# Graph attention with layer norm: the eight large additions and products at a group's end on GpSimd, and VectorE's comparisons one quad ahead

## The chip, the core and the metric

The kernel runs on one core of one Trainium2 chip. The metric is the device time of that core in microseconds (us): 1753.01 us, the median of three runs (1748.39 to 1753.73). One further execution was taken by the profiler.

## The reference

```python
x, adj: (8192, 128) f32, (8192, 8192) int32 of zeros and ones; 4 heads of 32 channels
Wh        = (x @ W.T) split by head
score_src = einsum('knd,kd->kn', Wh, a1);  score_dst = einsum('knd,kd->kn', Wh, a2)
e         = leaky_relu(score_src[:, :, None] + score_dst[:, None, :], 0.2)
e         = where(adj == 0, -inf, e)
alpha     = softmax(e, axis=-1)
h_prime   = einsum('kij,kjd->kid', alpha, Wh)
out       = layernorm(x + h_prime)      # over the 128 channels, eps 1e-5
```

## The kernel before

The exponential of the leaky ReLU is a product of a row factor and a column factor on either side of score_src + score_dst = 0, so for each pair of nodes the kernel needs only the edge and the sign of that sum. `step` holds the edges on the steep side, `rest` the other edges, both as one-byte matrices. TensorE multiplies `step` with `G` (three bf16 parts of the weighted values) and `rest` with `F` (two fp16 parts) and sums in six PSUM banks.

The output rows are taken in 16 groups of 512. For each group the kernel goes through 16 quads: 512 source nodes, four blocks of 128. One quad, numbered k over the whole kernel, goes through the engines so:

- SyncE loads one MB of `adj`, four buffers deep (`load_adj`).
- GpSimd makes `step` tiles of five of the 16 (block, head) pairs (line 325), then packs the `adj` block of quad k+2 to bytes (`take_edges`, line 302); that waits until TensorE has transposed quad k.
- TensorE transposes the packed block of quad k+2 into one of two PSUM banks (line 644) after VectorE has made `rest` of quad k, and before its own 64 `F` products of quad k.
- ScalarE makes nine `step` tiles (line 397).
- VectorE makes the last two (line 505), reading the transposed edges in PSUM. `take_step` then masks the 14 others with the edges in two instructions (lines 510 and 512), and `take_rest` makes `rest` by an exclusive or (line 522).
- TensorE multiplies (line 657): 64 products with `G` after `step_set`, 64 with `F` after `rest_set`.

`step` has four buffers and `rest` two. Every engine runs its own instruction list in the written order, and semaphores tie the lists together. Before the comparisons of quad k GpSimd also waits for `quad_past`, which VectorE raises at the end of a quad, k-1 times.

At the end of a group TensorE closes the six banks (line 672). ScalarE copies them to `late` after its comparisons of quad 1 of the next group (`take_sums`, line 381). VectorE then runs `finish` of the group before as a generator, one piece after each quad from quad 1 on: two additions of the partial sums (545, 546), a product with beta and an addition (549, 550), a product with alpha (553), an addition (556), maximum and reciprocal (559, 562), the product into `y` (566), the residual (571), the statistics (575, 580, 584). GpSimd raises the variance to the power -1/2 (306), VectorE makes the shift (589), ScalarE scales (`normalise`, 387), and SyncE stores. After the last group all this stands alone at the end. Every second group VectorE and ScalarE run through one body of a loop, TensorE and GpSimd have theirs unrolled.

Of the kernel before, what the change touches and what calls it, by code (L numbers as in the profile page):

```python
# [6 lines left out]
def gat_layernorm(nc, x, adj, W, a, out):  # L7
# [12 lines left out]
    ALU = mybir.AluOpType  # L20
# [3 lines left out]
    P = 128  # L24
    N, D_IN = x.shape
    HEADS, D_OUT = a.shape[0], a.shape[1] // 2
# [38 lines left out]
    with ctx:  # L65
# [3 lines left out]
        def sem(name):  # L69
            return ctx.enter_context(nc.semaphore(name))  # L70
# [93 lines left out]
        quad_past = sem("quad_past")  # L164
        pool_compared = sem("pool_compared")
        step_set = sem("step_set")
        rest_set = sem("rest_set")
        rest_done = sem("rest_done")
# [1 line left out]
        acc_act = sem("acc_act")  # L170
        res_loaded = sem("res_loaded")
        var_set = sem("var_set")
        rstd_set = sem("rstd_set")
        shift_set = sem("shift_set")
        y_set = sem("y_set")
# [16 lines left out]
        LEAD = 4  # L192


        SCALED = 14

        def done(n):
            return n + LEAD
# [72 lines left out]
        def _(pool):  # L271
# [25 lines left out]
            def take_edges(k):  # L297
# [3 lines left out]
                    pool.wait_ge(transposed, k - N8 + 1)  # L301
                nc.gpsimd.tensor_scalar(edge[:, k % N8], adj_t[:, k % NA], 1.0, -1.0, ALU.min, ALU.max).then_inc(edge_set, 1)  # L302

            def inverse_deviation(g):
                pool.wait_ge(var_set, done(g + 1))
                nc.gpsimd.tensor_tensor(rstd[:, :], mv[:, :, 1], half_t[:, :], ALU.pow).then_inc(rstd_set, 1)  # L306
# [108 lines left out]
        def _(dve):  # L415
# [79 lines left out]
            dve.wait_ge(part_set, done(3 * (JB // TJ)))  # L495
            dve.wait_ge(f_set, JB // TJ)

            def take_step(g, q, n):

                nth = at(dve, quad_no(g, q) + 1)  # L500
                if q == 0:
                    dve.wait_ge(s_loaded[n], 8 * (g + 2 - n))
                dve.wait_ge(transposed, nth)
                for b, h in DVE_TILES:
                    nc.vector.scalar_tensor_tensor(step_u8[:, q % NS, h, b // E, :, b % E], s_all[:, n, h],  # L505
                                                   d_neg[:, q * IB + b, h:h + 1], edgeT8[q % 2][:, b // E, :, b % E],
                                                   ALU.is_ge, ALU.logical_and)
                dve.wait_ge(act_compared, nth)
                dve.wait_ge(pool_compared, nth)
                nc.vector.scalar_tensor_tensor(step[:, q % NS, 0:HEADS - 1], edgeT[q % 2][:, 0:HEADS - 1], ONES,  # L510
                                               step[:, q % NS, 0:HEADS - 1], ALU.bitwise_and, ALU.bitwise_and)
                nc.vector.scalar_tensor_tensor(step[:, q % NS, HEADS - 1, 0:WORDS // U], edgeT[q % 2][:, HEADS - 1, 0:WORDS // U],  # L512
                                               ONES, step[:, q % NS, HEADS - 1, 0:WORDS // U], ALU.bitwise_and, ALU.bitwise_and
                                               ).then_inc(step_set, 1)


            def take_rest(g, q, waits=True):
# [7 lines left out]
            CHAIN0, CHAIN_STEP = links[0], 10  # L525

            def finish(g):

                got = [0]

                def then(ins):
                    got[0] += 1
                    ins.then_inc(dve_chain, 1)

                def wait_last():
                    dve.wait_ge(dve_chain, CHAIN0 + g * CHAIN_STEP + got[0])

                rows = bass.ds(g * IB, IB)

                def per_row(v, width):  # L540
                    return v.rearrange("p b h -> p (b h)").unsqueeze(2).to_broadcast([P, CHUNKS, width])

                top, low = acc_sb[:, :, 0:HC], acc_sb[:, :, BC:BC + HC]
                dve.wait_ge(acc_act, done((g + 2) * BANKS))
                nc.vector.tensor_tensor(low, low, acc_sb[:, :, BC + HC:CH], ALU.add)
                then(nc.vector.tensor_tensor(top, top, acc_sb[:, :, HC:2 * HC], ALU.add))
                yield
                wait_last()
                nc.vector.tensor_tensor(low, low, per_row(beta[:, rows, :], HC), ALU.mult)
                then(nc.vector.tensor_tensor(top, top, acc_sb[:, :, 2 * HC:BC], ALU.add))  # L550
                yield
                wait_last()
                then(nc.vector.tensor_tensor(top, top, per_row(alpha[:, rows, :], HC), ALU.mult))
                yield
                wait_last()
                then(nc.vector.tensor_tensor(top, top, low, ALU.add))
                yield
                wait_last()
# [3 lines left out]
                then(nc.vector.reciprocal(rden[:, :, :], rden[:, :, :]))  # L562
                yield
                wait_last()
                dve.wait_ge(stored, 16 * done(g))
                then(nc.vector.tensor_tensor(y.rearrange("p b (h c) -> p (b h) c", h=HEADS), top[:, :, 0:D_OUT],  # L566
                                             per_row(rden[:, :, :], D_OUT), ALU.mult))
                yield
                wait_last()
                dve.wait_ge(res_loaded, 16 * g + 16)  # L570
                then(nc.vector.tensor_tensor(y, y, res, ALU.add))  # L571
                yield
                wait_last()
# [11 lines left out]
                for _ in range(2):  # L585
                    yield
                assert got[0] == CHAIN_STEP
                dve.wait_ge(rstd_set, g + 1)
                nc.vector.scalar_tensor_tensor(shift[:, :], mv[:, :, 0], -1.0, rstd[:, :], ALU.mult, ALU.mult  # L589
                                               ).then_inc(shift_set, 1)  # L590

            def group(g, n, first=False, last=False):
                closing = iter(()) if first else finish(g - 1)
                for q in range(QUADS):
                    take_step(g, q, n)
                    take_rest(g, q, waits=not first or q >= NL)
                    if q > 0:
                        next(closing, None)
                    dve.sem_inc(quad_past, 1)  # L599
                for _ in closing:  # L600
                    pass

            group(0, 0, first=True)
            with dve.Fori(0, GROUPS // 2 - 1) as u:
                g = 2 * u + 1
# [110 lines left out]
```

## Time and profile before

| what | value |
|---|---|
| median of 3 runs | 1753.01 us |
| the profiled execution, its time | 1744.82 us |
| its span | 1743.0 us |
| VectorE busy | 1649.7 us, 95% |
| ScalarE busy | 1549.6 us, 89% |
| TensorE matmul busy | 1459.4 us, 84% |
| GpSimd busy | 1430.3 us, 82% |
| mean granted TensorE clock | 0.954 |

Busy time is the sum of the durations of an engine's instructions, so it tells how full the engine is. What one instruction costs in a row of them is read from start to start, since the next begins a little before the last has ended. Idle time with its releaser tells which semaphore ended it; "issue" is time in which the engine waited for nothing that the profile shows.

### The profile page before, as it was taken

The numbers are of one execution on the slowest core, as the hardware profiler recorded it, in microseconds if no ns is written. First come the engines' busy times: TensorE is split into PE (matmuls) and PEld (weight loads), VectorE is DVE, ScalarE is ACT, GpSimd is POOL, SyncE is SP. The second block draws the span as 40 slices with busy tenths as digits, with TensorE's granted clock in tenths as the row PEclk, the third lists the DMA queues.
The fourth block names the chain that finished last, engine by engine and source line by source line (L and its number), as shares of the span: only waits on it lengthen the run. The fifth ranks groups of instructions, "written<-read, shape, count | busy, mean of one in ns | idle before, by whom it ended". The sixth has DMA issues, their size and how long they took to land.

```text
span 1743.0 us, 80201 instructions
## 1 busy us (share of the span) xinstructions
PE 1459.4 (84%) x35235; PEld 1412.6 (81%) x35235; DVE 1649.7 (95%) x1856; ACT 1549.6 (89%) x2567; POOL 1430.3 (82%) x1582
## 2 busy tenths in 40 slices
PE   6306989989889889988889898998898998998886
PEld 4106988988888888988888888988888988888886
DVE  3697999999999999999999999999999999999997
ACT  3368999998999999899899999899998989999994
POOL 0039978989899888988899898989888898989983
PEclk9757999999999999999999999999999999999998
DMA  2505665656556575656557475555657565665530
GB/s 75 146 0 195 196 186 179 197 191 196 183 172 209 170 208 171 200 181 198 180 171 224 156 216 177 193 186 180 193 167 204 179 193 181 197 201 164 193 124 20
DMA packets 161762, 303.05 MB, mean 174 GB/s; under 512 B 9680, under 2 KB 22096, under 8 KB 161424
## 3 DMA queue, kind: packets, MB, share of 16 engines
q1 hardware_dynamic: 161424, 298.03, 54.5%
q8 instruction: 275, 4.51, 1.0%
q14 instruction: 63, 0.52, 0.1%
HBM read 293.67 MB, written 4.33 MB: 171 GB/s over the span
## 4 chain that ended last, share of the span: by engine, by line
DVE 39%; issue 29%; PE 17%; ACT 7%; POOL 4%; DMA 1%; DVEq 1%; SPq 0%; ACTq 0%; POOLq 0%
DVE step L510 17%; PE bank L657 14%; DVE step L505 12%; ACT step L397 6%; DVE step L512 3%; POOL step L325 3%; PE bank L644 1%; DMA xr<-in_x 1%; DVE F L488 1%; POOL edge L302 1%; DVE rest L522 1%; DVE stats L575 1%; ACT F L368 1%; DVE xr L571 1%; DVE xr L566 1%
## 5 line engine op out<-in xcount | busy, mean ns | idle before, releaser
L397 ACT ACTIVATE step<-s_all,sd 128x512 uint8<-128x512 f32 x2304 | 1423.1, 721 | 44.1 <-PE bank L657 43.9
L325 POOL TENSOR_SCALAR step<-s_all,sd 128x512 uint8<-128x512 f32 x1280 | 915.7, 734 | 113.1 <-DVEq L599 111.9
L657 PE MATMUL bank<-G,step 128*128 128x99 bf16 x16384 | 791.6, 209 | 138.8 <-DVE step L512 98.9
L657 PEld LDWEIGHTS bank<-G,step 128*128 128x128 fp8e4 x16384 | 751.8, 98 | 163.4 <-DVE step L512 122.2
L522 DVE SCALAR_TENSOR_TENSOR rest<-step,bank 128x2048 int32<-128x2048 int32 x256 | 585.7, 2288 | 10.1
L657 PE MATMUL bank<-F,rest 128*128 128x66 f16 x16384 | 556.5, 195 | 20.7 <-issue 20.7
L657 PEld LDWEIGHTS bank<-F,rest 128*128 128x128 fp8e4 x16384 | 537.1, 98 | 21.9 <-issue 21.9
L302 POOL TENSOR_SCALAR edge<-adj_t 128x2048 int8<-128x2048 int32 x256 | 484.6, 1893 | 58.4 <-PE bank L644 56.4
L510 DVE SCALAR_TENSOR_TENSOR step<-bank,step 128x1536 int32<-128x1536 int32 x256 | 447.5, 1748 | 3.2 <-ACT step L397 3.2
L505 DVE SCALAR_TENSOR_TENSOR step<-s_all,sd,bank 128x512 uint8<-128x512 f32 x512 | 358.9, 743 | 20.2 <-PE bank L644 9.9
L644 PE MATMUL bank<-identb,edge 128*128 128x128 bf16 x2048 | 159.1, 221 | 79.6 <-POOL edge L302 79.5
L644 PEld LDWEIGHTS bank<-identb,edge 128*128 128x128 bf16 x2048 | 125.1, 99 | 81.0 <-issue 80.0
L512 DVE SCALAR_TENSOR_TENSOR step<-bank,step 128x256 int32<-128x256 int32 x256 | 105.4, 412 | 0.0
L381 ACT COPY late<-bank 128x495 f32<-128x495 f32 x96 | 42.7, 552 | 59.7 <-PE bank L672 59.7
L286 POOL PARTITION_ALL_REDUCE d_max<-d_part x1 | 0.4, 389 | 62.6 <-DVE d_part L439 62.6
L433 DVE COPY G<-bank 128x256 f32 x32 | 13.4, 420 | 38.7 <-PE bank L637 38.7
L294 POOL TENSOR_TENSOR late<-late,G 128x528 f32<-128x528 f32 x8 | 10.5, 1336 | 44.7 <-ACT G L366 23.9
L387 ACT ACTIVATE xr<-xr,shift,rstd 128x128 f32<-128x128 f32 x64 | 26.2, 480 | 9.0 <-DVE shift L589 9.0
L306 POOL TENSOR_TENSOR rstd<-mv,half_t 128x4 f32<-128x4 f32 x16 | 16.3, 1019 | 21.7 <-DVE mv L584 21.7
L352 ACT COPY step<-bank 4x512 f32<-4x512 f32 x16 | 9.2, 574 | 24.5 <-PE bank L637 16.0
L366 ACT CAST G<-step 128x528 f32 x24 | 15.5, 648 | 15.8 <-DVE step L492 13.8
L366 ACT CAST G<-late 128x528 f32 x24 | 15.2, 647 | 13.6 <-DVE late L492 5.6
(78 smaller groups left out, 393.0 us busy)
## 6 DMA issues: line engine op xcount, KB each, us to landing
adj_t<-in_adj SPq DMA_DIRECT2D x512, 512.0 KB, 4.8
s_all<-sT_scratch SPq DMA_DIRECT2D x16, 1024.0 KB, 10.2
xr<-in_x SPq DMA_DIRECT2D x32, 256.0 KB, 3.1
out<-xr SPq DMA_DIRECT2D x16, 256.0 KB, 5.5
sT_scratch<-step SPq DMA_DIRECT2D x16, 8.0 KB
a_blk<-in_L_gnn_a SPq DMA_DIRECT2D x8, 0.1 KB, 1.7
step<-in_L_gnn_W SPq DMA_DIRECT2D x1, 64.0 KB, 1.8
```

Source lines behind the costliest of these rows:

```text
L302: nc.gpsimd.tensor_scalar(edge[:, k % N8], adj_t[:, k % NA], 1.0, -1.0, ALU.min, ALU.max).then_inc(edge_set, 1)
L325: last = nc.gpsimd.tensor_scalar(step_u8[:, k % NS, h, n // E, :, n % E], s_all[:, g % 2, h], STEEP, d_steep[:, q * IB + n, h:h + 1], ALU. ...
L366: last = nc.scalar.copy(G[:, blk, :, part, :], wide[n][:, :, :, 0])
L381: nc.scalar.copy(late[:, b * USED:b * USED + n_ch * CH], acc[b][:, 0:n_ch * CH]).then_inc(acc_act, 1)
L387: last = nc.scalar.activation(y[:, b], y[:, b], ACT.Identity, scale=rstd[:, b:b + 1], bias=shift[:, b:b + 1])
L397: last = nc.scalar.activation(step_u8[:, q % NS, h, b // E, :, b % E], s_all[:, n, h], ACT.Sigmoid, scale=STEEP, bias=d_steep[:, q * IB + ...
L505: nc.vector.scalar_tensor_tensor(step_u8[:, q % NS, h, b // E, :, b % E], s_all[:, n, h], d_neg[:, q * IB + b, h:h + 1], edgeT8[q % 2][:, ...
L510: nc.vector.scalar_tensor_tensor(step[:, q % NS, 0:HEADS - 1], edgeT[q % 2][:, 0:HEADS - 1], ONES, step[:, q % NS, 0:HEADS - 1], ALU.bitwi ...
L512: nc.vector.scalar_tensor_tensor(step[:, q % NS, HEADS - 1, 0:WORDS // U], edgeT[q % 2][:, HEADS - 1, 0:WORDS // U], ONES, step[:, q % NS, ...
L522: nc.vector.scalar_tensor_tensor(rest[:, q % NL], step[:, q % NS], ONES, edgeT[q % 2], ALU.bitwise_xor, ALU.bitwise_and).then_inc(rest_set, 1)
L644: last = nc.tensor.transpose(edgeT16[q % 2][:, u, b * P:(b + 1) * P], edge16[:, q % N8, b, u * P:(u + 1) * P], identb[:, :])
L657: last = nc.tensor.matmul(acc[k][:, col:col + width], matrix[:, h, n // E, b * P:(b + 1) * P, n % E], values[:, q * IB + n, h].rearrange(" ...
```

## The change

Eight `tensor_tensor` instructions of `finish` go from VectorE to GpSimd as `close(g, part)`, one after the `take_edges` of each of the quads in `CLOSING`. VectorE keeps maximum, reciprocal, statistics and shift, in quads 8, 11, 12 and 13. The power goes from quad 11 to quad 13 of GpSimd's list, `normalise` from quad 14 to quad 15 of ScalarE's. New semaphores (`low_set`, `top_set`, `rden_set`, `sum_set`) carry the chain across the two engines. GpSimd no longer waits for `quad_past`. VectorE's two comparisons are a function of their own, `compare`, that stands for quad q+1 between `take_step` and `take_rest` of quad q. Of the two masking instructions the small one comes first.

```diff
-        SCALED = 14
+        CLOSING = (2, 3, 4, 5, 6, 7, 9, 10)
+        SCALED = 15
+            def close(g, part):
+                if part == 0:
+                    pool.wait_ge(acc_act, done((g + 2) * BANKS))
+                    nc.gpsimd.tensor_tensor(low, low, acc_sb[:, :, BC + HC:CH], ALU.add).then_inc(low_set, 1)
+                elif part == 1:
+                    nc.gpsimd.tensor_tensor(top, top, acc_sb[:, :, HC:2 * HC], ALU.add).then_inc(top_set, 1)
...
+                elif part == 6:
+                    pool.wait_ge(rden_set, g + 1)
+                    pool.wait_ge(stored, 16 * done(g))
+                    nc.gpsimd.tensor_tensor(y.rearrange("p b (h c) -> p (b h) c", h=HEADS), top[:, :, 0:D_OUT],
+                                            per_row(rden[:, :, :], D_OUT), ALU.mult).then_inc(sum_set, 1)
+                else:
+                    pool.wait_ge(sum_set, 2 * g + 1)
+                    pool.wait_ge(res_loaded, 16 * g + 16)
+                    nc.gpsimd.tensor_tensor(y, y, res, ALU.add).then_inc(sum_set, 1)
...
                     k = quad_no(g, q)
-                    if k > 1:
-                        pool.wait_ge(quad_past, k - 1)
...
-                    if q == 11 and g > 0:
+                    if q in CLOSING and g > 0:
+                        close(g - 1, CLOSING.index(q))
+                    if q == 13 and g > 0:
                         inverse_deviation(g - 1)
+            for part in range(len(CLOSING)):
+                close(GROUPS - 1, part)
             inverse_deviation(GROUPS - 1)
...
                 for q in range(QUADS):
-                    take_step(g, q, n)
+                    take_step(g, q)
+                    if q + 1 < QUADS:
+                        compare(g, q + 1, n)
+                    elif not last:
+                        compare(g + 1, 0, 1 - n)
                     take_rest(g, q, waits=not first or q >= NL)
-                    if q > 0:
+                    if q >= 8:
                         next(closing, None)
-                    dve.sem_inc(quad_past, 1)
```

VectorE's list in quad 2 of a group before, with the piece of the group's end that follows it; L505 is a comparison, L510 and L512 mask, L522 makes `rest`.

```order
L505 SCALAR_TENSOR_TENSOR step<-s_all,sd,bank 128x512 [waits transposed]
L505 SCALAR_TENSOR_TENSOR step<-s_all,sd,bank 128x512
L510 SCALAR_TENSOR_TENSOR step<-bank,step 128x1536 [waits pool_compared,act_compared]
L512 SCALAR_TENSOR_TENSOR step<-bank,step 128x256
L522 SCALAR_TENSOR_TENSOR rest<-step,bank 128x2048 [waits rest_done,step_set]
L536 ISA
L549 ISA [waits dve_chain]
L549 TENSOR_TENSOR late<-late,beta 128x16x33
L550 TENSOR_TENSOR late<-late 128x16x33
```

The same place in the changed kernel; L559 masks, L547 are the comparisons of quad 3, L570 makes `rest` of quad 2.

```order
L559 SCALAR_TENSOR_TENSOR step<-bank,step 128x256 [waits pool_compared,act_compared,dve_compared]
L559 SCALAR_TENSOR_TENSOR step<-bank,step 128x1536
L545 REGISTER_ALU
L547 SCALAR_TENSOR_TENSOR step<-s_all,sd,bank 128x512 [waits transposed]
L547 SCALAR_TENSOR_TENSOR step<-s_all,sd,bank 128x512
L570 SCALAR_TENSOR_TENSOR rest<-step,bank 128x2048 [waits rest_done,step_set]
```

The large additions and products are gone from here, and the wait for the transposed edges of the next quad stands before `rest` of this one.

GpSimd's list in quads 1 and 2 of a group before:

```order
L325 TENSOR_SCALAR step<-s_all,sd 128x512 [waits rest_done,quad_past]
L325 TENSOR_SCALAR step<-s_all,sd 128x512 x4
L302 TENSOR_SCALAR edge<-adj_t 128x2048 [waits transposed,adj_loaded3]
L325 TENSOR_SCALAR step<-s_all,sd 128x512 [waits rest_done,quad_past]
L325 TENSOR_SCALAR step<-s_all,sd 128x512 x4
L302 TENSOR_SCALAR edge<-adj_t 128x2048 [waits transposed,adj_loaded0]
```

The changed kernel there, in quads 2 and 3; L320 and L322 are the first two parts of `close`.

```order
L364 TENSOR_SCALAR step<-s_all,sd 128x512 [waits rest_done]
L364 TENSOR_SCALAR step<-s_all,sd 128x512 x4
L308 TENSOR_SCALAR edge<-adj_t 128x2048 [waits transposed,adj_loaded0]
L320 TENSOR_TENSOR late<-late 128x16x33 [waits acc_act]
L364 TENSOR_SCALAR step<-s_all,sd 128x512 [waits rest_done]
L364 TENSOR_SCALAR step<-s_all,sd 128x512 x4
L308 TENSOR_SCALAR edge<-adj_t 128x2048 [waits transposed,adj_loaded1]
L322 TENSOR_TENSOR late<-late 128x16x33
```

Each part stands between the packing of quad k+2 and the comparisons of quad k+1, and `quad_past` is gone.

## Rows read from the trace of the kernel before

**Rows 1.** The page: busy time of each engine, and the chain by engine.
```profile
PE 1459.4 (84%) x35235; PEld 1412.6 (81%) x35235; DVE 1649.7 (95%) x1856; ACT 1549.6 (89%) x2567; POOL 1430.3 (82%) x1582
...
DVE 39%; issue 29%; PE 17%; ACT 7%; POOL 4%; DMA 1%; DVEq 1%; SPq 0%; ACTq 0%; POOLq 0%
```

**Rows 2.** Timeline of VectorE, one quad without an end piece: start, us, instruction.
```profile
908.87 1.40 DVE L505 SCALAR_TENSOR_TENSOR step<-s_all,sd,bank 128x512 uint8<-128x512 f32 x2
910.18 1.75 DVE L510 SCALAR_TENSOR_TENSOR step<-bank,step 128x1536 int32<-128x1536 int32 x1
911.85 0.41 DVE L512 SCALAR_TENSOR_TENSOR step<-bank,step 128x256 int32<-128x256 int32 x1
912.30 2.29 DVE L522 SCALAR_TENSOR_TENSOR rest<-step,bank 128x2048 int32<-128x2048 int32 x1
914.50 1.40 DVE L505 SCALAR_TENSOR_TENSOR step<-s_all,sd,bank 128x512 uint8<-128x512 f32 x2
```

**Rows 3.** Line 672, TensorE closing the banks: durations, first and last start.
```profile
L672 PE MATMUL bank<-zeros,identb x96: 166/167/169, 237.1 to 1728.5; 128*128 128x2 bf16 x96
```

**Rows 4.** Timeline of VectorE after the last quad.
```profile
1729.74 0.71 DVE L545 TENSOR_TENSOR late<-late 128x528 f32<-128x528 f32 x1 [3.93 <-ACT late L381]
...
1733.95 0.17 DVE L559 TENSOR_SCALAR rden<-late 128x16 f32<-128x16 f32 x1
...
1734.44 0.69 DVE L566 TENSOR_TENSOR xr<-late,rden 128x512 f32<-128x512 f32 x1
...
1735.89 0.87 DVE L575 BATCH_NORM_STATS2 stats<-xr 128x6 f32<-128x128 f32 x4
...
1737.21 0.17 DVE L584 TENSOR_SCALAR mv<-mv 128x4 f32<-128x4 f32 x1
1738.52 0.16 DVE L589 SCALAR_TENSOR_TENSOR shift<-mv,rstd 128x4 f32<-128x4 f32 x1 [1.14 <-POOL rstd L306]
```

**Rows 5.** Timeline of GpSimd in the middle of the kernel.
```profile
841.98 4.39 POOL L325 TENSOR_SCALAR step<-s_all,sd 128x512 uint8<-128x512 f32 x5 [0.31 <-DVEq L599]
...
902.63 1.02 POOL L306 TENSOR_TENSOR rstd<-mv,half_t 128x4 f32<-128x4 f32 x1
...
908.87 3.38 POOL L325 TENSOR_SCALAR step<-s_all,sd 128x512 uint8<-128x512 f32 x5
...
914.09 3.38 POOL L325 TENSOR_SCALAR step<-s_all,sd 128x512 uint8<-128x512 f32 x5
```

**Rows 6.** Line 294 on GpSimd: ns of one at least, median, at most.
```profile
L294 POOL TENSOR_TENSOR late<-late,G x8: 1149/1222/1670, 86.2 to 132.5; 128x528 f32<-128x528 f32 x8
```

**Rows 7.** Timeline of ScalarE.
```profile
834.22 2.67 ACT L381 COPY late<-bank 128x495 f32<-128x495 f32 x6 [4.23 <-PE bank L672]
...
906.45 5.63 ACT L397 ACTIVATE step<-s_all,sd 128x512 uint8<-128x512 f32 x9 [0.63 <-PE bank L657]
911.98 1.63 ACT L387 ACTIVATE xr<-xr,shift,rstd 128x128 f32<-128x128 f32 x4
```

**Rows 8.** Timeline of TensorE, from quad 1 of a group on.
```profile
841.72 0.66 PE L657 MATMUL bank<-G,step 128*128 128x99 bf16 x11
847.38 3.79 PE L657 MATMUL bank<-G,step 128*128 128x99 bf16 x53 [5.00 <-issue]
851.00 0.61 PE L644 MATMUL bank<-identb,edge 128*128 128x128 bf16 x8
...
853.42 3.01 PE L657 MATMUL bank<-G,step 128*128 128x99 bf16 x64
856.26 0.61 PE L644 MATMUL bank<-identb,edge 128*128 128x128 bf16 x8
...
858.68 3.01 PE L657 MATMUL bank<-G,step 128*128 128x99 bf16 x64
```

**Rows 9.** Waits: engine and line, what it waited for: us, times, longest.
```profile
POOL step L325 <- DVEq L599: 111.9, 88, 3.5
...
PE bank L657 <- issue: 58.6, 27, 5.6
```

More of the change, by code:

```diff
@@ L163, in gat_layernorm @@
         act_compared = sem("act_compared")
-        quad_past = sem("quad_past")
         pool_compared = sem("pool_compared")
+        dve_compared = sem("dve_compared")
         step_set = sem("step_set")
@@ L172, in gat_layernorm @@
         var_set = sem("var_set")
+        low_set = sem("low_set")
+        top_set = sem("top_set")
+        rden_set = sem("rden_set")
+        sum_set = sem("sum_set")
         rstd_set = sem("rstd_set")
@@ L302, in take_edges, with per_row @@
                 nc.gpsimd.tensor_scalar(edge[:, k % N8], adj_t[:, k % NA], 1.0, -1.0, ALU.min, ALU.max).then_inc(edge_set, 1)
+            def close(g, part):
+                top, low = acc_sb[:, :, 0:HC], acc_sb[:, :, BC:BC + HC]
+                def per_row(v, width):
+                    return v.rearrange("p b h -> p (b h)").unsqueeze(2).to_broadcast([P, CHUNKS, width])
+                rows = slice(g * IB, (g + 1) * IB)
+                if part == 0:
[3 more added lines that the diff above has]
+                    nc.gpsimd.tensor_tensor(top, top, acc_sb[:, :, HC:2 * HC], ALU.add).then_inc(top_set, 1)
+                elif part == 2:
+                    pool.wait_ge(low_set, 2 * g + 1)
+                    nc.gpsimd.tensor_tensor(low, low, per_row(beta[:, rows, :], HC), ALU.mult).then_inc(low_set, 1)
+                elif part == 3:
+                    pool.wait_ge(top_set, 4 * g + 1)
+                    nc.gpsimd.tensor_tensor(top, top, acc_sb[:, :, 2 * HC:BC], ALU.add).then_inc(top_set, 1)
+                elif part == 4:
+                    pool.wait_ge(top_set, 4 * g + 2)
+                    nc.gpsimd.tensor_tensor(top, top, per_row(alpha[:, rows, :], HC), ALU.mult).then_inc(top_set, 1)
+                elif part == 5:
+                    pool.wait_ge(top_set, 4 * g + 3)
+                    pool.wait_ge(low_set, 2 * g + 2)
+                    nc.gpsimd.tensor_tensor(top, top, low, ALU.add).then_inc(top_set, 1)
+                elif part == 6:
[7 more added lines that the diff above has]
+                    nc.gpsimd.tensor_tensor(y, y, res, ALU.add).then_inc(sum_set, 1)
             def inverse_deviation(g):
@@ L496, in _, with compare @@
             dve.wait_ge(f_set, JB // TJ)
-            def take_step(g, q, n):
-                nth = at(dve, quad_no(g, q) + 1)
+            def compare(g, q, n):
                 if q == 0:
                     dve.wait_ge(s_loaded[n], 8 * (g + 2 - n))
-                dve.wait_ge(transposed, nth)
+                dve.wait_ge(transposed, at(dve, quad_no(g, q) + 1))
                 for b, h in DVE_TILES:
-                    nc.vector.scalar_tensor_tensor(step_u8[:, q % NS, h, b // E, :, b % E], s_all[:, n, h],
-                                                   d_neg[:, q * IB + b, h:h + 1], edgeT8[q % 2][:, b // E, :, b % E],
-                                                   ALU.is_ge, ALU.logical_and)
+                    last = nc.vector.scalar_tensor_tensor(step_u8[:, q % NS, h, b // E, :, b % E], s_all[:, n, h],
+                                                          d_neg[:, q * IB + b, h:h + 1], edgeT8[q % 2][:, b // E, :, b % E],
+                                                          ALU.is_ge, ALU.logical_and)
+                last.then_inc(dve_compared, 1)
@@ L508, in take_step @@
+            def take_step(g, q):
+                nth = at(dve, quad_no(g, q) + 1)
+                dve.wait_ge(dve_compared, nth)
                 dve.wait_ge(act_compared, nth)
                 dve.wait_ge(pool_compared, nth)
[L510 to L514, printed above, removed]
+                for part in ((slice(HEADS - 1, HEADS), slice(0, WORDS // U)), (slice(0, HEADS - 1), slice(0, WORDS))):
+                    last = nc.vector.scalar_tensor_tensor(step[:, q % NS, part[0], part[1]], edgeT[q % 2][:, part[0], part[1]],
+                                                          ONES, step[:, q % NS, part[0], part[1]],
+                                                          ALU.bitwise_and, ALU.bitwise_and)
+                last.then_inc(step_set, 1)
@@ L523, in take_rest @@
                                                ALU.bitwise_xor, ALU.bitwise_and).then_inc(rest_set, 1)
-            CHAIN0, CHAIN_STEP = links[0], 10
+            CHAIN0, CHAIN_STEP = links[0], 3
             def finish(g):
@@ L536, in wait_last @@
                     dve.wait_ge(dve_chain, CHAIN0 + g * CHAIN_STEP + got[0])
[L538 to L558, printed above, removed]
+                top = acc_sb[:, :, 0:HC]
+                dve.wait_ge(top_set, 4 * g + 4)
                 then(nc.vector.tensor_scalar(rden[:, :, :], top[:, :, D_OUT].rearrange("p (b h) -> p b h", h=HEADS),
@@ L561, in finish @@
                 wait_last()
[L562 to L573, printed above, removed]
+                nc.vector.reciprocal(rden[:, :, :], rden[:, :, :]).then_inc(rden_set, 1)
+                for _ in range(3):
+                    yield
+                dve.wait_ge(sum_set, 2 * g + 2)
                 for b in range(IB):
@@ L584, in finish @@
                 nc.vector.tensor_scalar(mv[:, :, 1], mv[:, :, 1], EPS, None, ALU.add).then_inc(var_set, 1)
-                for _ in range(2):
+                assert got[0] == CHAIN_STEP
+                for _ in range(1):
                     yield
-                assert got[0] == CHAIN_STEP
                 dve.wait_ge(rstd_set, g + 1)
@@ L594, in group @@
                 for q in range(QUADS):
-                    take_step(g, q, n)
+                    take_step(g, q)
[3 more added lines that the diff above has]
+                        compare(g + 1, 0, 1 - n)
                     take_rest(g, q, waits=not first or q >= NL)
-                    if q > 0:
+                    if q >= 8:
                         next(closing, None)
-                    dve.sem_inc(quad_past, 1)
                 for _ in closing:
                     pass
+            compare(0, 0, 0)
             group(0, 0, first=True)
```

## Prediction, written before the changed kernel was run

> **What bounds the kernel now.** I read the page first: VectorE is busy for 95% of the span and heads the chain, while ScalarE, TensorE and GpSimd have 11 to 18% left [rows 1]. Then VectorE's timeline. Between pieces of a group's end a quad takes 914.50 - 908.87 = 5.63 us, back to back: comparisons 1.31, the large mask 1.67, the small mask 0.45, `rest` 2.20 [rows 2]. The small mask lasts 0.41 us, and instructions here overlap by about 0.08, so it should take 0.33; the other 0.12 us is the wait of `rest` for `step_set`, raised by the instruction just ahead. A group: the banks are closed from 237.1 to 1728.5 us, six times a group, and the six of one group lie 1.7 us apart, so 15 groups take 1489.7 us and one takes 99.3 [rows 3]. Sixteen quads are 90.1 of these; 9.2 remain for the group's end and for waits. So VectorE sets the pace, and a microsecond taken from it counts until the next engine is full.
>
> **What the change takes from VectorE.** The eight moved instructions take 1733.95 - 1729.74 = 4.21 and 1735.89 - 1734.44 = 1.45 us in the tail, 5.7 together [rows 4]; in the groups they also lose some to waits. The 0.12 us for `step_set` goes from each quad, since 1.3 us of comparisons now stand between: 1.9 per group. What stays is 0.49 (maximum, reciprocal), 1.49 (from 1735.89 to the end of the one at 1737.21) and 0.16 for the shift, 2.1 in all [rows 4]. VectorE alone then needs 16 x 5.51 + 2.1 = 90.3 us a group, and I add 0.3 for the loop's turn (an estimate): 90.6.
>
> **What it gives to GpSimd.** A quad there takes 914.09 - 908.87 = 5.22 us, 83.5 for sixteen, and the power 1.0 [rows 5]. Eight `tensor_tensor` come on top. The nearest row is line 294 with the same 16 runs of 33 numbers per partition: 1.15 us at least, 1.22 median, 1.67 at most, the longer ones while VectorE itself had two-input work [rows 6]. None of that is beside the moved parts now, so I take 1.15: 9.2 us. Below it the price could only fall to VectorE's own 0.7 (5.66/8, [rows 4]); above, to 1.67. GpSimd alone: 83.5 + 1.0 + 9.2 = 93.7 us, more than VectorE. Its present waits for `quad_past`, 111.9 us [rows 9], go, but they were not what held VectorE, so I count nothing for them; their cover is that GpSimd still cannot pack quad k+2 before quad k is transposed.
>
> The row at 841.98 shows five comparisons in 4.39 us instead of 3.38, while VectorE ran its two-input additions [rows 5]. The Trainium skill (SBUF — State Buffer, Who interferes with whom) says that a VectorE instruction with two SBUF inputs holds off a GpSimd one that reads SBUF, and that one with a single SBUF input does not. By that rule, the trace agrees (1.0 us), the stretching goes with the move, and the price of a part is its undisturbed one; without the rule I would take the median, 1.22, and the group would be 0.6 us longer.
>
> **What the new order costs.** Call T the end of a quad's masks on VectorE. TensorE needs 2.84 us for 64 products with `G`, 0.45 for transposes and 1.97 for `F`, 5.26 in all when it never waits (853.42 to 858.68 in [rows 8]; the transposes are complete 0.61 after they start). In the new list `rest` is ready at T + 1.3 + 2.2 = T + 3.5, the transposes for quad q+2 are done at T + 4.2, and VectorE wants them at T + 5.5. So 1.3 us of room is left. Before, VectorE wanted them only after the next `rest`: TensorE had them at T + 3.5 and VectorE came at T + 7.9, 4.4 us of room, and 5.6 with an end piece of 1.2 ahead. That matters because TensorE stands still once per group, in the `G` products of quad 1: 5.00 us in the row shown, and the 53 products behind it take 851.00 - 847.38 = 3.62 us where 53/64 of 2.84 is 2.35, so 1.3 more [rows 8]. All such stops come to 58.6 us [rows 9], 3.9 per group. Nearly all of it used to be hidden in those 5.6 us. Now TensorE is late by 3.6 (the large one) + 1.3 = 4.9, of which VectorE sees 4.9 - 1.3 = 3.6 us. VectorE: 90.6 + 3.6 = 94.2.
>
> GpSimd meets the same stop, since packing quad 5 waits for the transposes of quad 3. How far ahead it is decides. From part 7 (quad 10) on it gains 0.3 us per quad on VectorE, and 2.1 from what VectorE kept, and pays 1.0 for the power, so at quad 3, after the first part, it is about 2.1 us ahead of the masks. Its packing could then start at T1 + 8.9 - 2.1 = T1 + 6.8 (T1 is T of quad 1), and the transposes are done at T1 + 4.2 + 4.9 = T1 + 9.1: 2.3 us lost. Another 0.3 I give to the power, whose variance now comes only in quad 12. GpSimd: 93.7 + 2.6 = 96.3 us a group. The parts cost it 0.85 us per quad net against VectorE, so the lead is gone by about quad 8, and from there VectorE waits for `pool_compared`, about 2 us a group in all. That is the same sum seen from VectorE: 94.2 + 2.1 = 96.3.
>
> ScalarE: nine tiles take 911.98 - 906.45 = 5.53 us, sixteen quads 88.5, copies of the banks 2.5 (2.67 less the overlap), scaling 1.5 [rows 7]; 92.5 without waits. It comes under 96.3 with 3.8 us for its waits at the banks (4.23 in the row shown) and for the shift, which now comes only two quads ahead of use.
>
> **The sum**, against the profiled execution's 1744.8 us (span 1743.0): 15 groups by 99.3 - 96.3 = 3.0 each, -45; group 0, which has no end work, by 16 x 0.11 (ScalarE's 5.53 is next), -2; the tail, where eight parts at 1.15 plus about 0.05 of semaphore each replace 5.7, +4. Together -43, 1702. The median of the runs shown lies 8.2 us above the profiled execution, so I forecast 1753 - 43 = 1710 us. Low end: a GpSimd that never waits, 93.7, gives -84 - 2 + 4 = -82, 1671. High end with the parts at 1.67: +4.2 a group and +4 in the tail makes +24, 1777; that needs the disturbed price where nothing disturbs, so I let the range reach only half of that way.
>
> **Rivals.**
> 1. The stop of TensorE is hidden after all (GpSimd comes to it with no lead, or the stop moves to a place with more room). GpSimd then gives 94 to 94.5 a group, -75, 1678. For it: packing at zero lead begins at T3 - 0.2 - 1.9 (T3 that of quad 3), well behind the transposes. Against: the trace shows this stop in the same quad of nearly every group. 0.2.
> 2. ScalarE becomes the bound and keeps its waits. Its rows show 4.23 us at the banks and 0.63 in one quad [rows 7]; 92.5 + 4.2 + several 0.6 is 98.5, and the gain is 15 x 0.8 + 2 - 4 = 10, 1743. If it stays at 4.23 alone it is 96.7, my forecast. Against: its waits are those of an engine that is ahead, and they shrink when the others speed up. 0.1.
> 3. Slower. GpSimd cannot store up any lead, because packing is tied to the transposes two quads back and these to `rest`. Then every part counts in full against VectorE: 8 x (1.15 - 0.3) = 6.8, with the stop 3.6, 90.6 + 10.4 = 101.0 a group, +26 - 2 + 4 = +28, 1781. It decides from 8.6 us of waits per group on VectorE (99.2 less 90.6). For it: 1.3 us of room instead of 4.4. Against: the ring lets GpSimd be nearly one quad ahead, and 88 waits on `quad_past` show that it gets there [rows 9]. 0.08.
> 4. A part costs much more than line 294, as a product with a broadcast operand or into `y` might; at 1.55 us a part the gain is gone, at 1.67 it is the 1777 above. 0.07.
>
> The Trainium skill (GPSIMD Engine Reference, Elementwise — side-by-side cycle accounting) speaks against such a move: it gives GpSimd about 2.6 cycles per element with two inputs and calls VectorE twice as fast. Its figures make 528 elements an estimated 1.14 us; line 294's 1.15 agrees. By it the two engines' sum grows, and the move pays only through GpSimd's idle share.
>
> **Chances.** Forecast 0.55; rivals 0.2, 0.1, 0.08, 0.07. A measurement of this kernel tells about 0.3%, 5 us, from no change. Faster by more: forecast, the first, most of the second: 0.83. Within: 0.06. Slower: 0.11. The range, 1680 to 1748, takes in most of the first two rivals.
>
> **What would show it.** Right: a group of 96 to 97 us; quads of 5.5 us on VectorE with no gap ahead of `rest`; parts of 1.12 to 1.25 us; comparisons on GpSimd at 3.38 everywhere; VectorE waiting for TensorE's transposes about once a group, 2 to 5 us, near quad 3, and for GpSimd in quads 7 to 11; GpSimd the fullest engine with VectorE. Wrong: parts above 1.4 us (rival 4), ScalarE ending VectorE's waits (2), waits of VectorE over 8 us a group (3), or no wait for transposes at all (1).

## The result, and the profile after

The changed kernel takes 1712.59 us, the median of four runs (1706.65 to 1714.83), against 1751.72 us of the kernel before beside it; the ratio is 0.9774, 95% interval [0.9753, 0.9795]. The forecast was 1710 us. The two profiled executions lie 1744.8 - 1714.8 = 30 us apart, less than the medians' 39: the one of before was faster than all four of its runs, the one of after was the slowest of its four. What follows explains those 30 us.

The page after, answering [rows 1]:

```profile
PE 1462.5 (85%) x35235; PEld 1411.8 (82%) x35235; DVE 1558.9 (91%) x1728; ACT 1544.6 (90%) x2567; POOL 1521.7 (89%) x1710
...
POOL 34%; DVE 21%; PE 20%; issue 15%; ACT 7%; DMA 1%; DVEq 0%; SPq 0%; ACTq 0%; POOLq 0%
```

GpSimd has taken the head of the chain. The banks of the groups are now closed like this (line 672 of before is line 697), answering [rows 3]:

```profile
L697 PE MATMUL bank<-zeros,identb x96: 166/167/169, 241.9 to 1694.8; 128*128 128x2 bf16 x96
```

1694.8 - 241.9 - 1.7 over 15 is 96.7 us a group; it was 99.3 and was forecast at 96.3. Group 0 ends 4.8 us later than before, the tail behind the last bank went from 14.5 to 18.2 us. The 15 groups bring -38.5 us, and -38.5 + 4.8 + 3.7 gives the 30.

VectorE in a quad without an end piece, answering [rows 2] (start, duration; two merged masks, two comparisons, `rest`):

```profile
824.37 2.08 DVE L559 SCALAR_TENSOR_TENSOR step<-bank,step 128x256 int32<-128x256 int32 x2
826.37 1.39 DVE L547 SCALAR_TENSOR_TENSOR step<-s_all,sd,bank 128x512 uint8<-128x512 f32 x2
827.68 2.27 DVE L570 SCALAR_TENSOR_TENSOR rest<-step,bank 128x2048 int32<-128x2048 int32 x1
829.88 2.08 DVE L559 SCALAR_TENSOR_TENSOR step<-bank,step 128x256 int32<-128x256 int32 x2
```

A quad is 5.51 us, as forecast, and nothing stands ahead of `rest`. Three of the eight parts on GpSimd, by line: shortest, median, longest in ns, answering [rows 6]:

```profile
L320 POOL TENSOR_TENSOR late<-late x16: 1122/1142/1153, 250.5 to 1696.1; 128x528 f32<-128x528 f32 x16
...
L335 POOL TENSOR_TENSOR late<-late x16: 1317/1348/1367, 289.2 to 1701.7; 128x528 f32<-128x528 f32 x16
...
L344 POOL TENSOR_TENSOR xr<-xr x16: 1261/1281/1286, 307.6 to 1704.7; 128x512 f32<-128x512 f32 x16
```

The eight sum to 9.3 us (1.06 to 1.35 each), 9.2 was forecast. A product with a broadcast operand is no dearer than a sum. The comparisons on GpSimd fell from 734 to 699 ns in the mean.

TensorE's stop, at its worst, on the three engines that feel it (one fence for each engine; the brackets give the idle time and what ended it). TensorE:

```profile
250.25 0.43 PE L682 MATMUL bank<-G,step 128*128 128x99 bf16 x6
256.13 5.01 PE L682 MATMUL bank<-G,step 128*128 128x99 bf16 x58 [5.45 <-issue]
260.94 1.05 PE L669 MATMUL bank<-identb,edge 128*128 128x128 bf16 x8
```

VectorE:

```profile
252.01 2.08 DVE L559 SCALAR_TENSOR_TENSOR step<-bank,step 128x256 int32<-128x256 int32 x2
262.02 1.41 DVE L547 SCALAR_TENSOR_TENSOR step<-s_all,sd,bank 128x512 uint8<-128x512 f32 x2 [7.93 <-PE bank L669]
```

GpSimd:

```profile
251.58 3.39 POOL L364 TENSOR_SCALAR step<-s_all,sd 128x512 uint8<-128x512 f32 x5
262.15 1.89 POOL L308 TENSOR_SCALAR edge<-adj_t 128x2048 int8<-128x2048 int32 x1 [7.18 <-PE bank L669]
```

VectorE wants the transposed edges of quad 3 at 254.1 and gets them at 262.0; GpSimd cannot pack before the same transposes are done. The stop also slows what follows it: from 256.1 to 261.0 the granted clock was 0.50, which is 1.2 GHz, after TensorE had stood still for 5.45 us, and the 58 products behind the stop took 4.8 us (260.94 - 256.13) where 58/64 of 2.84 is 2.6. In a group with a 2.69 us stop (TensorE goes on at 846.39) the clock behind it was 1.00, and the waits are 1.31 and 0. The waits in all (us, times, longest), answering [rows 9]:

```profile
DVE step L547 <- PE bank L669: 72.3, 30, 7.9
PE bank L682 <- issue: 70.6, 43, 5.4
...
POOL edge L308 <- PE bank L669: 44.1, 22, 7.2
...
POOL rstd L348 <- DVE mv L605: 8.2, 16, 1.6
...
POOL xr L339 <- DVE rden L591: 7.4, 16, 1.2
...
DVE step L559 <- POOL step L364: 6.6, 9, 0.9
```

The last row is the one that was not foreseen: VectorE hardly waits for GpSimd's comparisons. What took that time shows in quad 8. VectorE, then GpSimd:

```profile
881.63 1.46 DVE L588 TENSOR_SCALAR rden<-late 128x16 f32<-128x16 f32 x1
883.12 0.25 DVE L591 RECIPROCAL rden<-rden 128x16 f32<-128x16 f32 x1
```
```profile
881.15 1.91 POOL L308 TENSOR_SCALAR edge<-adj_t 128x2048 int8<-128x2048 int32 x1
883.46 1.06 POOL L339 TENSOR_TENSOR xr<-late,rden 128x512 f32<-128x512 f32 x1 [0.40 <-DVE rden L591]
```

The maximum over 16 numbers took 0.17 us before [rows 4]; now it ends just as GpSimd's packing does, at 883.1. Its median is 1452 ns, that of the shift 897 (187 before). Not every group pays that: in the mean of the 15 groups the maximum lasts 1.07 us longer than before and the shift 0.58.

### The profile page after: what moved, and what is told of

Read it like the earlier page. It is cut to its first block, busy times and chain, and to the rows that moved or that the text cites. A ratio compares the mean times of both kernels' runs of the same rounds, so it can differ in the third digit from the quotient of the medians.

```text
span 1713.0 us, 79627 instructions
## 1 busy us (share of the span) xinstructions
PE 1462.5 (85%) x35235; PEld 1411.8 (82%) x35235; DVE 1558.9 (91%) x1728; ACT 1544.6 (90%) x2567; POOL 1521.7 (89%) x1710
## 4 chain that ended last, share of the span: by engine, by line
POOL 34%; DVE 21%; PE 20%; issue 15%; ACT 7%; DMA 1%; DVEq 0%; SPq 0%; ACTq 0%; POOLq 0%
POOL step L364 20%; PE bank L682 17%; POOL edge L308 10%; DVE rest L570 7%; DVE step L559 6%; ACT step L440 5%; DVE step L547 5%; PE bank L669 2%; DMA xr<-in_x 1%; DVE F L531 1%; POOL xr L344 1%; DVE stats L596 1%; ACT F L411 1%; POOL late L328 1%; POOL late L325 1%
## 5 line engine op out<-in xcount | busy, mean ns | idle before, releaser
L364 POOL TENSOR_SCALAR step<-s_all,sd 128x512 uint8<-128x512 f32 x1280 | 865.8, 699 | 0.0
L570 DVE SCALAR_TENSOR_TENSOR rest<-step,bank 128x2048 int32<-128x2048 int32 x256 | 583.4, 2279 | 0.0
L559 DVE SCALAR_TENSOR_TENSOR step<-bank,step 128x256 int32<-128x256 int32 (+1 forms) x512 | 532.2, 1080 | 12.8 <-POOL step L364 6.6
L308 POOL TENSOR_SCALAR edge<-adj_t 128x2048 int8<-128x2048 int32 x256 | 485.3, 1896 | 44.3 <-PE bank L669 44.1
L547 DVE SCALAR_TENSOR_TENSOR step<-s_all,sd,bank 128x512 uint8<-128x512 f32 x512 | 358.2, 742 | 72.6 <-PE bank L669 72.3
L669 PEld LDWEIGHTS bank<-identb,edge 128*128 128x128 bf16 x2048 | 121.0, 99 | 138.0 <-issue 80.6
L424 ACT COPY late<-bank 128x495 f32<-128x495 f32 x96 | 41.9, 526 | 11.2 <-PE bank L697 11.2
L320 POOL TENSOR_TENSOR late<-late 128x528 f32<-128x528 f32 x16 | 18.3, 1141 | 11.8 <-ACT late L424 11.8
L588 DVE TENSOR_SCALAR rden<-late 128x16 f32<-128x16 f32 x16 | 18.7, 1168 | 10.9 <-POOL late L335 10.9
```

Of the source, the lines that this page charges most:

```text
L424: nc.scalar.copy(late[:, b * USED:b * USED + n_ch * CH], acc[b][:, 0:n_ch * CH]).then_inc(acc_act, 1)
L547: last = nc.vector.scalar_tensor_tensor(step_u8[:, q % NS, h, b // E, :, b % E], s_all[:, n, h], d_neg[:, q * IB + b, h:h + 1], edgeT8[q % ...
L559: last = nc.vector.scalar_tensor_tensor(step[:, q % NS, part[0], part[1]], edgeT[q % 2][:, part[0], part[1]], ONES, step[:, q % NS, part[0 ...
L669: last = nc.tensor.transpose(edgeT16[q % 2][:, u, b * P:(b + 1) * P], edge16[:, q % N8, b, u * P:(u + 1) * P], identb[:, :])
```

## The experiments

All were timed in three rounds beside the kernel before; ratios are to it, and differences in us between two versions are taken from their ratios unless a subtraction is written out. Of each edit the central lines are shown; `...` marks lines left out between them. "Stop" is short for TensorE's standing still, once a group.

**order_only**: the kernel before with the new order on VectorE alone (the small mask first, as in the changed kernel).

```diff
-                    take_step(g, q, n)
+                    take_step(g, q)
+                    if q + 1 < QUADS:
+                        compare(g, q + 1, n)
+                    elif not last:
+                        compare(g + 1, 0, 1 - n)
                     take_rest(g, q, waits=not first or q >= NL)
```

> The kernel before with only the new order on VectorE (comparisons of quad q+1 between the masks and rest of quad q); the group's end stays on VectorE and GpSimd keeps its wait for quad_past. Theory A (the stop of TensorE once a group, which the old order hid, now reaches VectorE): the 1.9 us per group saved at step_set are given back by a wait of VectorE for the transposes of about 2 us, group 99 to 99.8 us, 1745 to 1758 us, nearly no change. Rival B (the order is a gain by itself): 15 x 1.9 + 2 = 30 us less, 1720 us.

1747.64 us, 0.9986 [0.9969, 1.0004]: no change that can be told. VectorE's waits for the transposes rose from 9.9 us to

```profile
DVE step L505 <- PE bank L655: 39.8, 17, 5.4
```

which is about what 16 x 1.9 at `step_set` had given, 30 us. Theory A holds.

**move_only**: the changed kernel with VectorE's old order.

```diff
-                    take_step(g, q)
-                    if q + 1 < QUADS:
-                        compare(g, q + 1, n)
-                    elif not last:
-                        compare(g + 1, 0, 1 - n)
+                    take_step(g, q, n)
```

> The changed kernel with VectorE's old order (comparisons of quad q just ahead of its masks); the eight additions and products are on GpSimd and quad_past is gone. Theory A (GpSimd is full at 93.7 us a group plus its waits, and the old order leaves VectorE 4.4 us of room for TensorE's stop): VectorE needs 92.5 us alone, GpSimd 93.7 + 1.5 to 2.5, group 95.3 to 96.5, 1700 to 1715 us, as fast as the changed kernel or a little faster. Rival B (the order brings its 1.9 us per group): about 98.5 a group, 1740 us.

1719.98 us, 0.9824 [0.9806, 0.9841], 5 us above the expected span. So the move brings 1.8 points of the 2.3, and the order about half a point on top, far less than rival B's.

**with_quad_past**: the changed kernel with GpSimd's wait for `quad_past` put back.

```diff
                     k = quad_no(g, q)
+                    if k > 1:
+                        pool.wait_ge(quad_past, k - 1)
```

> The changed kernel with GpSimd's wait for quad_past put back. Theory A (GpSimd's lead is bounded anyway by the transposes two quads back): the lead it may store falls by at most about 2 us; GpSimd is the full engine, so each wait counts: 0 to 2 us a group, 1712 to 1742 us. Rival B (the pacing was not binding): 1712, no wait on DVEq in the trace. A third view (the removed pacing is what made the change pay, as GpSimd needs its lead for the eight parts): over 3 us a group, above 1757 us.

1718.71 us, 0.9811 [0.9789, 0.9833]. That is about 6 us above the changed kernel, at the edge of what the intervals tell apart. GpSimd's comparisons never waited for `quad_past`:

```profile
L367 POOL TENSOR_SCALAR step<-s_all,sd 128x512 uint8<-128x512 f32 x1280 | 865.4, 698 | 0.0
```

That is the sign of rival B: taking this wait out was not what made the change pay.

**split_s**: the load of a group's scores in four parts.

```diff
-            def load_s(g, n):
-                src = sT_v[g].unsqueeze(0).to_broadcast([P, HEADS, ROWS])
-                sync.dma_start(s_all[:, n], src).then_inc(s_loaded[n], 16)
+            def load_s(g, n, heads=range(HEADS)):
+                for h in heads:
+                    src = sT_v[g, h:h + 1].unsqueeze(0).to_broadcast([P, 1, ROWS])
+                    sync.dma_start(s_all[:, n, h:h + 1], src).then_inc(s_loaded[n], 16)
...
-                    if q == 6 and g + 1 < GROUPS:
+                    if q in (6, 8, 10, 12) and g + 1 < GROUPS:
```

> The changed kernel with the one load of a group's scores (s_all, 1 MB) split by head into four loads, after the adjacency loads of quads 6, 8, 10 and 12. Theory A (TensorE's stop in quad 1 is instruction fetch that queues behind this load): the stops fall from 65 us to under 25 in all and no longer sit in quad 1; VectorE's 72 us of waits for transposes and GpSimd's 44 fall by more than half; group 94 to 95, 1680 to 1695 us. Rival B (the stop belongs to that place in TensorE's instruction list whatever the DMAs do): same stops, 1712 us. Rival C (the small loads are slower in sum): 1720 us.

1676.11 us, 0.9580 [0.9559, 0.9602]. Waits and bank closings:

```profile
DVE step L560 <- POOL step L365: 23.5, 36, 0.9
...
PE bank L683 <- issue: 14.0, 26, 1.6
DVE step L548 <- PE bank L670: 13.3, 10, 5.3
```
```profile
L698 PE MATMUL bank<-zeros,identb x96: 166/167/169, 236.1 to 1654.9; 128*128 128x2 bf16 x96
```

The long stops are gone, and a group is (1654.9 - 236.1 - 1.7) / 15 = 94.5 us. That is GpSimd's list with no wait for TensorE in the groups: 83.5 + 1.0 + 9.3, and 0.8 for its waits for the reciprocal and the variance, 94.6. Theory A holds for the load; that instruction fetch is what waits behind it is not shown. The stop cost the changed kernel 2.2 us a group, and 5.8 us in group 0, which ends at 236.1 instead of 241.9. The mean granted clock rose from 0.955 to 0.968; this is a part of the stop's price.

**before_split_s** and **order_only_split_s**: the same edit on the kernel before, and on order_only.

> The kernel before with the score load split by head into four loads, after the adjacency loads of quads 6, 8, 10 and 12; nothing else. Theory A (the old order hid TensorE's stop almost whole, and the new order is worth its 1.9 us per group once the stop is gone): 98.4 to 99.3 a group, 1735 to 1750 us, so that order_only_split_s (1717.6) lies 20 to 30 us below it. Rival B (the new order is worth nothing in itself): 1718 us, as with the new order.

> The kernel before with the new order on VectorE, and with the score load split by head into four loads, after the adjacency loads of quads 6, 8, 10 and 12. Theory A (the order alone gave nothing because TensorE's stop took back what step_set gave): without the stop the 1.9 us per group appear, and the part of the stop that was not hidden; group 96.4 to 97.2, 1700 to 1718 us. Rival B (the order has no gain, its 1.9 us are lost for another reason, as by waits of TensorE): group 98.5, 1738 us.

before_split_s: 1734.12 us, 0.9915 [0.9898, 0.9931], a hair under the expected span. order_only_split_s: 1717.60 us, 0.9826 [0.9795, 0.9856], at its upper end. So the order alone is worth 16 us without the stop, less than the 20 to 30 expected, and nothing with it. And the stop costs the kernel before 15 us, the changed kernel 0.9774 - 0.9580, 34 us.

**move_only_split_s**: move_only with the load in four parts.

> The changed kernel with VectorE's old order, and with the score load split as in split_s. Theory A (GpSimd is full at 94.4 us a group once the stop is gone, and VectorE's old order needs 92.5 plus 1.5 to 2 us in which its maximum and its shift wait for GpSimd): 94.4 to 95.5 a group, 1676 to 1692 us, little behind split_s's 1676. Rival B (the order brings its 1.9 us per group in full): 96.3, 1705 us.

1680.34 us, 0.9605 [0.9589, 0.9621]. That is 4 us above split_s, and the intervals overlap: with GpSimd full, the new order gives little even without the stop. With the stop it gave 9 (0.9824 - 0.9774).

**late_s**: the changed kernel, the load whole but at quad 10 of SyncE's list.

```diff
-                    if q == 6 and g + 1 < GROUPS:
+                    if q == 10 and g + 1 < GROUPS:
```

> The changed kernel with the one undivided score load issued after the adjacency load of quad 10 instead of quad 6. Theory A (the load makes the stop): TensorE's long stops move from quad 1 to about quad 5 of a group, with their sum (60 us) unchanged; GpSimd has less lead there and waits less for the transposes, 1700 to 1713 us. Rival B (the stop belongs to quad 1 of TensorE's list): the stops stay in quad 1 and the time at 1712 us.

1681.79 us, 0.9611 [0.9595, 0.9628], far below either expectation. The long stops ended 31 to 36 us after a group's last bank instead of 11 to 15, and they sum to less. The longest, on TensorE, and GpSimd beside it:

```profile
652.52 4.01 PE L682 MATMUL bank<-G,step 128*128 128x99 bf16 x46 [4.76 <-issue]
656.33 0.84 PE L669 MATMUL bank<-identb,edge 128*128 128x128 bf16 x8
```
```profile
651.20 3.40 POOL L364 TENSOR_SCALAR step<-s_all,sd 128x512 uint8<-128x512 f32 x5
657.33 1.89 POOL L308 TENSOR_SCALAR edge<-adj_t 128x2048 int8<-128x2048 int32 x1 [2.73 <-PE bank L669]
```

All waits:

```profile
PE bank L682 <- issue: 51.1, 42, 4.8
...
DVE step L547 <- PE bank L669: 39.3, 26, 6.3
```

This stop of 4.76 us holds GpSimd for 2.73. Stops of 3.34 to 3.62 us held it for 1.8 to 2.6 in the changed kernel, and those of 3.35 and 3.38 here not at all; its waits for transposes fall from 44.1 to 9.8 us. So the load makes the stop, and its place decides much of what it costs. GpSimd's rows fit the prediction's picture of a lead that the parts use up: at the worst stop of the changed kernel it was through with its comparisons at 254.97, 1.2 us before TensorE went on, with one part made; here at 654.60, 2.1 us after, with five made. How much of the gain comes from that, and how much from the shorter stops, no run tells. The direction was expected; that 28 of the stop's 34 us would go was not.

**gpsimd_extra** and **vectore_extra**: the changed kernel with work added on one engine whose result is used by nothing; first GpSimd's edit, behind the dots VectorE's.

```diff
+                    if q == 8 and g > 0:
+                        nc.gpsimd.tensor_tensor(spare[:, :, :],
+                                                alpha[:, :, :].rearrange("p j h -> p (j h)").unsqueeze(1).to_broadcast([P, 2, JB * HEADS]),
...
+                for b in range(IB):
+                    nc.vector.bn_stats(spare[:, b], y[:, b])
```

> The changed kernel with one more addition of 512 numbers per partition (about 1.1 us) on GpSimd in quad 8 of each of 15 groups; its result is used by nothing. Theory A (GpSimd is the full engine of the changed kernel): all of it counts, 15 x 1.1 = 16 us, 1728 us. Rival B (VectorE with the waits for transposes sets the pace): 1712 to 1717 us.

> The changed kernel with the four bn_stats of a group made twice on VectorE (0.87 us more per group, the copy used by nothing). Theory A: it stands in quad 11, where VectorE else waits for GpSimd, so 0 to 5 us, 1712 to 1717 us. Rival B (VectorE sets the pace): 16 x 0.87 = 14 us, 1726 us.

gpsimd_extra: the addition took 1.29 us, 19 in all, and the kernel 1732.20 us, 0.9900 [0.9871, 0.9930]: 22 us more, so all of it counts. vectore_extra: 1721.93 us, 0.9841 [0.9825, 0.9858], 12 of the 14 us added. That is outside Theory A's 1712 to 1717 and under rival B's 1726. The trace shows the way it takes, on GpSimd:

```profile
POOL rstd L349 <- DVE mv L608: 20.1, 16, 2.4
```

against 8.2 us. The statistics are not beside GpSimd's work: the power stands in its list in quad 13 and waits for them with all comparisons of the later quads behind it. GpSimd is the full engine, and this is one of the places where VectorE's time enters its list.

**split_s_max**: split_s with the maximum on GpSimd.

```diff
                     nc.gpsimd.tensor_tensor(top, top, low, ALU.add).then_inc(top_set, 1)
+                    pool.wait_ge(top_set, 4 * g + 4)
+                    nc.gpsimd.tensor_scalar(rden[:, :, :], top[:, :, D_OUT].rearrange("p (b h) -> p b h", h=HEADS),
+                                            TINY, None, ALU.max).then_inc(max_set, 1)
```

> split_s with the maximum of the row sums (16 numbers per partition) on GpSimd after the sixth part, so that VectorE keeps only the reciprocal there. Theory A (VectorE's 0.17 us maximum took 1.45 us because GpSimd's edge packing held the shared SBUF port, which also delayed the seventh part on GpSimd by 0.4 us; GpSimd is the full engine): GpSimd pays about 0.15 and gets 0.4 back, group 94.1 to 94.4, 1671 to 1677 us; VectorE's extra 1.3 us are gone, and the reciprocal stays at 0.25. Rival B (VectorE sets the pace even here): 16 x 1.3 = 20 us less, 1655 us. Rival C (the port delay moves to the reciprocal): 1676 us with a reciprocal above 1 us.

1672.92 us, 0.9560 [0.9544, 0.9576]. The reciprocal stays at 0.25 us; VectorE's 1.3 us turn into waits for the comparisons (42.0 us instead of 23.5), and the group stays at 94.4. Theory A holds; in time the version can't be told from split_s. Its median is the lowest of all versions.

**split_s_max_residual**: this with the residual's addition back on VectorE, in quad 11 ahead of the statistics; the eighth part leaves GpSimd's list.

```diff
+                dve.wait_ge(sum_set, g + 1)
+                dve.wait_ge(res_loaded, 16 * g + 16)
+                then(nc.vector.tensor_tensor(y, y, res, ALU.add))
+                wait_last()
```

> split_s_max with the residual's addition moved back to VectorE, ahead of its statistics in quad 11. Theory A (GpSimd is full, 94.3 us a group, with a residual of 1.28; VectorE has about 2 to 3 us left): group 93.0 to 93.3, ScalarE's 92.5 next; 1655 to 1662 us. Rival B (VectorE's two-input addition and GpSimd hold each other off at the shared port and give back what was moved): 1671 to 1677 us.

1762.83 us, 1.0075 [1.0058, 1.0092], slower than the kernel before by 0.75%. VectorE, then GpSimd:

```profile
908.99 6.89 DVE L593 TENSOR_TENSOR xr<-xr 128x512 f32<-128x512 f32 x1
915.91 0.87 DVE L596 BATCH_NORM_STATS2 stats<-xr 128x6 f32<-128x128 f32 x4
```
```profile
908.23 1.89 POOL L310 TENSOR_SCALAR edge<-adj_t 128x2048 int8<-128x2048 int32 x1
910.10 3.38 POOL L365 TENSOR_SCALAR step<-s_all,sd 128x512 uint8<-128x512 f32 x5
913.44 1.90 POOL L310 TENSOR_SCALAR edge<-adj_t 128x2048 int8<-128x2048 int32 x1
923.00 1.03 POOL L349 TENSOR_TENSOR rstd<-mv,half_t 128x4 f32<-128x4 f32 x1 [7.67 <-DVE mv L605]
```

An addition that takes 0.69 us in the tail of this run lasted 6.89, and so in 13 of the 15 groups (6.16 and 6.39 us in the other two). It ended 0.55 us after GpSimd's last instruction at 915.3, through seven of them that followed each other without a gap, and none of the seven was stretched. GpSimd then stood 7.67 us for the variance, in all

```profile
POOL rstd L349 <- DVE mv L605: 117.3, 16, 7.7
```

against 8.2 us in split_s_max. 109 us of new waits less 15 x 1.28 for the part that left GpSimd is 90, and the kernel lost 1762.83 - 1672.92 = 90 us. Rival B holds, in a size that nobody expected, and one-sided: only VectorE was held off. Why it was held through all seven is open: GpSimd also ran without a gap beside a 1.98 us product of the kernel before, which came in behind one instruction (below).

## Why the prediction was right, and where its steps were off

- **VectorE's quad**: 5.51 us, as worked out. **The parts**: 9.3 us against 9.2; the sum `top + low` and the residual at 1.3 us were above line 294's best case, the products below it. **GpSimd's comparisons** at 3.38 us everywhere, as forecast.
- **The stop reaches GpSimd**: forecast 2.3 us a group, measured 96.7 - 94.5 = 2.2 by split_s. This was the step on which the forecast and its first rival (1678 us) parted. The rival's time is that of split_s and late_s; its condition, a GpSimd that comes to the stop with no lead, is what the row at 651.20 of late_s shows. The range began at 1680 us, above this rival's 1678 and the low end of 1671, so a time that the prediction itself gave a chance of 0.2 lay outside it.
- **The stop reaches VectorE**: forecast 3.6 us a group, measured (72.3 - 5.3) / 16 = 4.2; the 5.3 is the wait at the very start, which the kernel before has too. That the old order "hid nearly all of it" was too strong: before_split_s gains 1 us a group.
- **VectorE waits about 2 us a group for the comparisons**: wrong place, right sum. The waits are 6.6 us in the whole kernel. Instead the maximum takes 1.3 and the shift 0.7 us longer in the median group, 2.0, and 1.6 in the mean, while GpSimd holds them off. The prediction had applied the port rule to the eight moved parts only and not to what stayed on VectorE. With the 4.2 and the 0.4 of waits for GpSimd, 90.6 + 6.2 = 96.8 closes VectorE's sum. That the right sum came out of the wrong term is luck. Without the stop the holds cost nothing that can be told: split_s_max takes the 1.3 away. In the changed kernel that was not run.
- **Group 0**: forecast -2 us, measured +4.8. It has the stop too (2.53 us at 159.8, and VectorE waits 3.74 behind it), which I had left out; without it group 0 ends at 236.1 in split_s, 1.0 us earlier than before. **The tail**: forecast +4, measured +3.7.
- **A group**: 96.3 forecast, 96.7 measured, 15 x 0.4 = 6 us. With group 0's 7 us these are the 13 by which the profiled pair (-30) misses the sum (-43). The medians, -39, are nearer because the two profiled executions lie at opposite ends of their runs. So it is in part luck that 1710 came within 3 us of 1712.59; the mechanism and a group's length carry the forecast, the last few us don't.
- **Rival 2** (ScalarE keeps its waits): its waits at the banks fell from 59.7 to 11.2 us, but those for the shift rose:

```profile
ACT xr L430 <- DVE shift L610: 68.7, 16, 12.8
```

about 3.7 us a group besides the tail's 12.8. That was foreseen in kind. It sets no pace: 92.5 + 3.7 is just under GpSimd's 96.7, and in split_s, where a group is 94.5, these waits fall to 40.8 us in all. **Rivals 3 and 4** are out: VectorE's waits and holds come to 6.2 us a group, short of 8.6, and the parts are at 1.16 in the mean.

That TensorE lacked instructions during the stop, as its "issue" label suggests, is argued and not shown: in the runs with and without stops the instruction transfers have the same size and share (275 packets, 1.0%). During the stops shown the DMA engines were busy to a mean share of 1.00 (changed kernel, 250.7 to 256.1), 0.96 (late_s, 647.8 to 652.5) and 0.77 (kernel before, 842.3 to 847.3), against 0.54 to 0.56 over the spans; that fits anything that must come by DMA, and settles nothing more. Shown is that the load of the scores makes the stop and its place moves it.

## What to carry to other kernels

Before work moves from a full engine to one with a fifth of its time free, add up the receiving engine's whole list with the new work: that sum, plus its waits, was the forecast. Then ask of every transfer or stop that was hidden by room in the old order how much room is left, and in which quad the receiving engine meets it: here splitting one load in four was worth 34 us on the changed kernel and 15 on the one before. And a two-input instruction of VectorE beside a full GpSimd should be timed where it will stand: here one of 0.7 us took 6.9.

## What the runs showed of the hardware

The Trainium skill (SBUF — State Buffer, Who interferes with whom) describes the port that VectorE and GpSimd share as a lock that the later one waits for until the first one's instruction ends. It counts among its users VectorE instructions with two inputs in SBUF, as the shift and the residual are, and also `tensor_scalar`, which is the maximum's kind, where it enters a mode that uses both ports. This exception was missing in the prediction, which had one input in SBUF as free. The traces agree for the maximum (0.17 us became 1.45, up to the end of one GpSimd instruction) and go beyond it for the residual (0.7 became 6.9, over seven GpSimd instructions in a row). Why the shift of four numbers slipped in between two of them (818.04 to 818.94) and the addition of 512 did not, no run here settles. Nor do gaps alone explain it. In the kernel before, VectorE's product at 857.65 lasted 1.98 us, to 0.57 us after GpSimd's packing ended, and GpSimd's next comparisons followed at once, stretched to 3.83 us. VectorE, then GpSimd:

```profile
857.65 1.98 DVE L553 TENSOR_TENSOR late<-late,alpha 128x528 f32<-128x528 f32 x1
```
```profile
857.17 1.89 POOL L302 TENSOR_SCALAR edge<-adj_t 128x2048 int8<-128x2048 int32 x1
859.04 3.83 POOL L325 TENSOR_SCALAR step<-s_all,sd 128x512 uint8<-128x512 f32 x5
```

There VectorE got in right behind the packing. In split_s_max_residual it did not, at 910.1.
